# Attention with a softmax row passed through memory: when its reciprocals are taken, in what pieces they are written, and where the next weights are issued

## The reference

```python
scores = jnp.einsum('bhqd,bhkd->bhqk', q, k) / np.sqrt(Q_HEAD)
attn = jax.nn.softmax(scores, axis=-1)
o = jnp.einsum('bhqk,bhkv->bhqv', attn, v)
out = jnp.einsum('bhsv,Hv->bsH', o, Wo) + bo
```

## Time and profile before

| | |
|---|---|
| median of 3 runs | 3141.04 us (3134.56 to 3143.93) |
| the profiled execution, its own time | 3140.14 us |
| its span, first to last instruction | 3138.5 us |
| mean granted TensorE clock | 0.837 |
| PE busy | 2249.6 us (72%) |
| DVE busy | 1706.5 us (54%) |
| ACT busy | 1467.1 us (47%) |
| POOL busy | 516.1 us (16%) |

### The profile page before, as it was taken

How to read it: one execution, slowest core, us unless ns; L and a number is a source line. 1 busy time by engine, 2 the same in 40 slices (tenths; PEclk the granted TensorE clock), 3 DMA queues, 4 the chain that set the end, 5 groups by cost and what they waited for, 6 DMA issues and landing times. The chain is left out here.

```text
span 3138.5 us, 36938 instructions
## 1 busy us (share of the span) xinstructions
PE 2249.6 (72%) x11014; PEld 1759.9 (56%) x11014; DVE 1706.5 (54%) x2716; ACT 1467.1 (47%) x2616; POOL 516.1 (16%) x831
## 2 busy tenths in 40 slices
PE   8776767677776767676767677676767676676769
PEld 7555555555555555555655555555555555554557
DVE  6555555555555555554555555555555555554555
ACT  4454544444444445454444444444545444444434
POOL 3111111111111111111111111111211111111130
PEclk9888888878887888888888878887888888788789
DMA  5201010000001000101010010001010110101011
GB/s 205 74 21 26 21 26 21 22 25 21 27 20 27 20 27 20 26 21 26 22 24 24 21 26 20 27 20 27 21 27 21 26 21 20 27 20 26 18 56 45
DMA packets 123461, 95.20 MB, mean 30 GB/s; under 512 B 75008, under 2 KB 97568, under 8 KB 123424
## 3 DMA queue, kind: packets, MB, share of 16 engines
q1 hardware_dynamic: 119328, 86.33, 10.7%
q0 software_dynamic: 4096, 8.40, 1.0%
HBM read 83.95 MB, written 10.75 MB: 30 GB/s over the span
## 5 line engine op out<-in xcount | busy, mean ns | idle before, releaser
L766 ACT ACTIVATE PTH<-X 128x512 fp32r<-128x512 f32 x1024 | 565.7, 595 | 475.4 <-PE X L675 469.5
L817 DVE TENSOR_TENSOR PTL<-X,PTH 128x512 f16<-128x512 f32 x1024 | 664.6, 684 | 124.0 <-ACT PTH L766 119.8
L662 PE MATMUL O<-qaH,weff 128*128 128x512 f32 x128 | 100.2, 783 | 836.4 <-DVE onorm L849 822.1
L833 DVE TENSOR_REDUCE mx<-S 128x1 f32<-128x1024 f32 x512 | 622.9, 1217 | 57.8 <-PE S L695 57.5
L675 PE MATMUL X<-ident,prob 128*128 128x128 f32 x4096 | 628.9, 304 | 18.2 <-DVE PTL L817 15.6
L675 PEld LDWEIGHTS X<-ident,prob 128*128 128x128 f32 x4096 | 556.5, 160 | 144.5 <-issue 95.2
L849 DVE TENSOR_TENSOR onorm<-O,recip_row 128x512 f32<-128x512 f32 x128 | 88.5, 691 | 981.5 <-DMA recip_row<-row_scratch 981.5
L781 ACT ACTIVATE prob<-S,shift 128x1024 f32<-128x1024 f32 x512 | 572.1, 1117 | 0.0
L662 PEld LDWEIGHTS O<-qaH,weff 128*128 128x128 f32 x128 | 36.6, 286 | 890.1 <-DMA weff<-weff_scratch 797.4
L693 PE MATMUL S<-kvTH,qeH 128*128 128x512 f32 x1024 | 478.1, 467 | 1.6 <-DVE qeL L822 1.6
L798 ACT ACTIVATE onormH<-onorm 128x512 fp32r<-128x512 f32 x128 | 80.7, 631 | 805.0 <-DVE onorm L849 805.0
(11 more groups left out here) (201 smaller groups left out, 2139.4 us busy)
## 6 DMA issues: line engine op xcount, KB each, us to landing
recip_row<-row_scratch SPq DMA_DIRECT2D x128, 256.0 KB, 5.1
weff<-weff_scratch SPq DMA_DIRECT2D x128, 192.0 KB, 5.0
wv<-in_wv POOLq DMA_DIRECT2D x128, 64.0 KB, 2.1
raw<-in_raw SPq DMA_DIRECT2D x8, 772.0 KB, 6.6
weff_scratch<-w_split SPq DMA_DIRECT2D x8, 768.0 KB, 4.9
x<-in_x SPq DMA_DIRECT2D x4, 1024.0 KB, 6.8
x_all<-in_x SPq DMA_DIRECT2D x3, 1024.0 KB, 6.6
out<-y SPq DMA_DIRECT2D x3, 1024.0 KB, 4.2
```

Of the source, the lines that this page charges most:

```text
L662: mm(O[:], w[:, 0, :], keep["qaH"][:, tok], start=True, stop=False)
L766: nc.scalar.activation(PTH[p][:, part:part + 4, unit * P:(unit + 1) * P], X[:, k % 2, :].rearrange("p (k c) -> p k c", k=4), ACT.Copy).the ...
L817: v.tensor_tensor(PTL[p][at], X[:, k % 2, :].rearrange("p (k c) -> p k c", k=4), f32(PTH[p][at]), ALU.subtract).then_inc(low_out, 1)
L833: v.reduce_max(mx[:, col:col + 1], S[:, u % 2, :], AX.X).then_inc(max_ready, 1)
```

## The change

Four things change, all in `attention`:

1. DVE takes the reciprocals of head g-1 in quarter 1 of body g, in front of `low_q`, in place of quarter 2.
2. The scratch row is laid out by partition, then quarter (`"(p u) -> p u"`). Each partition's four numbers are now one piece of 16 bytes, 128 pieces, where there were 512 pieces of 4 bytes.
3. `onorm` reads `recip_row` in that layout: for a fixed quarter, its elements lie 16 bytes apart. `O` and `onorm` are addressed as before.
4. SP issues `load(g + 2)` in front of the wait for the reciprocals, not behind the read of the row.

```diff
             def body(g, b, h, par):
+                if exists(g + 2):
+                    load(g + 2, two_on[h] if not isinstance(g, int) else dram["weff_h"][(h + 2) % NH], par)
                 if exists(g - 1):
 
                     last = 1 - par
 
                     sp.wait_ge(recip_ready, g)
-                    with nc.allow_non_contiguous_dma(reason="512 numbers, turned from columns into a row"):
-                        sp.dma_start(dram["row"][last].rearrange("(u p) -> p u", p=P),
-                                     recip[:, last * UN:(last + 1) * UN]).then_inc(recip_out, 16)
+                    sp.dma_start(dram["row"][last].rearrange("(p u) -> p u", u=UN),
+                                 recip[:, last * UN:(last + 1) * UN]).then_inc(recip_out, 16)
                     sp.wait_ge(recip_out, 16 * g)
                     sp.dma_start(recip_row[last][:], dram["row"][last].partition_broadcast(P)).then_inc(row_in[last], 16)
-                if exists(g + 2):
-                    load(g + 2, two_on[h] if not isinstance(g, int) else dram["weff_h"][(h + 2) % NH], par)
...
-                        v.tensor_tensor(onorm[:], O[:], recip_row[par][:], ALU.mult).then_inc(onorm_ready, 1)
-                    if u == 1 and on and exists(g + 1):
-                        low_q(g + 1, h + 1 if not isinstance(g, int) else (h + 1) % NH, 1 - par)
-                    if u == 2 and one:
+                        v.tensor_tensor(onorm[:].rearrange("k (u p) -> k u p", u=UN), O[:].rearrange("k (u p) -> k u p", u=UN),
+                                        recip_row[par][:].rearrange("k (p u) -> k u p", u=UN), ALU.mult).then_inc(onorm_ready, 1)
+                    if u == 1 and one:
                         dve.wait_ge(probs_ready, 4 * g)
                         if not isinstance(g, int) or g >= 3:
                             dve.wait_ge(recip_out, 16 * (g - 2))
                         v.reciprocal(recip[:, (1 - par) * UN:(2 - par) * UN],
                                      rs[:, (1 - par) * UN:(2 - par) * UN]).then_inc(recip_ready, 1)
+                    if u == 1 and on and exists(g + 1):
+                        low_q(g + 1, h + 1 if not isinstance(g, int) else (h + 1) % NH, 1 - par)
```

## The result

The changed kernel takes 2000.7 us (1997.69 to 2001.29, 4 runs) where the kernel before took 3138.28 beside it: a ratio of 0.6372, 95% interval 0.6359 to 0.6385. The forecast was 2000. The span of the profiled execution is 1998.9 us.

A forecast was written before the change was run, and what follows sets the result against it. The row's chain, 22.7 us a head, would fall to 12.7, leaving PE's 13.66 as bound. With 0.14 added, 122.45 + 126 x 13.8, about 12, 124.4 and the small remainders give 2000 us; range 1970 to 2180.

The forecast's parts named there:

- What bounds: Waits for the row, `onorm` and `weff` are one gap; a head's period is a closed DVE, write, read, DVE chain, 22.71 us.
- The floor of 13.66 us: Sum of PE's four quarters at full clock: what a head costs where nothing waits for the row.
- The addition of 0.14: Added us per head for meetings of engines with little to spare, giving 13.8 us.
- The write: SP's write of the row to memory: 3.75 us with 128 pieces, between ends of 2.0 and 8.98.
- 2.0 + 7.0 / 4: The write's estimate: 2.0 us fixed, 7.0 us going with the pieces, of which a quarter remain.
- The read: Read of the row back from memory: unchanged at 5.1 us, between 3.2 and 5.6.
- The reciprocal's move: DVE's reciprocals in quarter 1 come 4.9 us earlier; their 0.17 us in front of `low_q` costs nothing.
- The load: Load of `weff` issued before the write: without that, its 797 us of waits become the next stall once the row is quicker.
- `onorm` with steps: `onorm` on DVE takes up to 1.06 us, not 0.69, but hidden; without cover 47 us in all.
- the copy's row: Profile row of a DVE copy spreading 512 elements by 16 bytes: 1.055 us against 0.684 plain; used to size `onorm`.
- The tail: From body 128's first transposes to the last `onorm`: about 12 us, where it was 26.1.
- a rival: Row still a little late: a write of 5 to 6 us gives 14.3 to 15.0 a head, about 2115 us; chance 0.12.

The follow-up runs named there:

- b_loadfront: The kernel before with only the load of `weff` moved in front of the write: 2989.94 us, ratio 1.0008.
- a_plain_onorm: The changed kernel with `onorm` reading the row without 16-byte steps, so reciprocals meet the wrong queries and only time counts: 1982.65 us, ratio 0.6322.
- x_spaced: The changed kernel plus one unread scratch write between write and read, 512 pieces of 4 bytes, 64 bytes apart: 2000.97 us, one execution.
- x_all16: The changed kernel plus one unread scratch write between write and read, 512 pieces of 4 bytes, 16 bytes apart: 2006.44 us, one execution.
- a_pieces4: The changed kernel with the write in 512 pieces of 4 bytes again and `onorm` without steps: 2467.48 us, ratio 0.7867.
- x_one: The changed kernel plus one unread scratch write of one column, 128 pieces of 4 bytes close together in 512 bytes: 2404.05 us, one execution.
- b_quarter1: The kernel before with only the reciprocals moved to quarter 1: 2340.37 us, ratio 0.7836, on a chip where the kernel before takes 2986.95.
- a_quarter2: The changed kernel with the reciprocals back in quarter 2, behind `low_q`: 1996.89 us, ratio 0.6368.
- a_loadback: The changed kernel with the load of `weff` back behind the read of the row: 2002.16 us, ratio 0.6382.

## Why the prediction was right

- *What bounds.* One chain, not three costs: right. b_loadfront shows it best: taking one of the three waits away changed its name and no time.
- *The floor of 13.66 us.* It was read from four quarters at full clock, two of them from the first heads. a_plain_onorm, where neither the row nor `onorm`'s steps are in the way, has transposes from body to body at (1844.00 - 122.47) / 126 = 13.66 us. The floor was right to 0.01.
- *The addition of 0.14.* Guessed, for meetings of engines in general, and the sum came out (13.80): that it did to the hundredth is luck. It now has a cause: at each of the 56 turns of the loop, with `onorm`'s longer time, 0.23 us in quarter 0 and 0.08 in quarter 1, or 56 x 0.31 / 126 = 0.14 a head.
- *The write.* 3.75 us forecast, 1.9 to landing and 1.44 of waiting measured, below the low end of 2.0. The step that failed is 2.0 + 7.0 / 4: it shared the time out by the number of pieces. The runs show closeness in its place. Memory completing 512 pieces, as the prediction had it, is not what the time goes with: 512 pieces at 64 bytes land in 2.6 us. That this didn't move the result is due to the slack, which is not large: 4.5 us from the write's issue to the read's gave 2001 us (x_spaced), 5.6 us gave 2006 (x_all16), both with a quicker read of 3.3 to 3.4.
- *The read.* 5.1 taken, 4.2 measured. It is longer (5.1) in a_pieces4, behind the close pieces. It does not simply follow the length of the write just ahead: in x_one that is 7.2 us and the read 3.5.
- *The reciprocal's move.* Its 4.9 us were sized rightly (5.05 in b_quarter1), and its new wait costs nothing. But the text let it stand as part of the gain. With the pieces of 16 bytes it brings nothing, since the chain is at the floor without it: a_quarter2. And its place in front of `low_q` is not quite free, as the prediction had it: 0.08 us in quarter 1 at each turn, 3.8 us between the two kernels.
- *The load.* Wrong. The prediction said that `weff` would become the next stall if the load kept its place. a_loadback shows no such stall. The step missed that the load follows the read, and that the read itself moves forward: it is issued 999.56 - 993.81 = 5.75 us behind the body's `onorm`, where it was 1507.03 - 1489.81 = 17.2.
- *`onorm` with steps.* The length was right (1.06 forecast, 1.07 measured), by the copy's row; "hidden" was not. With the turn of the loop it costs 2000.7 - 1982.65 = 18 us; 47 had been named as the price without cover. The cover was counted in a body inside the loop; at the turn it is shorter.
- *The tail.* About 12 us from the last body's transposes to the last `onorm`; 1874.4 - 1861.93 = 12.5 measured.
- *A slip in a rival.* A write of 5 us gives 3.84 + 5 + 5.1 = 13.9 us a head, not 14.3; only one of 6 us is clearly over the floor.

The Trainium skill, SBUF — State Buffer, section Specifications (TRN2), warned of a penalty for each new 16-byte line. The traces agree: `onorm` takes 1.07 us with the steps and 0.69 without, and that is what separates a_plain_onorm from the changed kernel. The Trainium skill, DMA: Bandwidth & Descriptors, section Anatomy of one DMA, written for the path that POOL issues, makes the receipt most of the fixed part and lets the fixed part scale with nothing. That most of such a write is spent behind its packets agrees with the earlier trace rows: they are gone by 1499.5, and SP goes on at 1507.03. That it scales with nothing does not hold for these writes, which SP issues: 1.44 to 8.98 us of waiting for at most 2 KB.

## What to carry to other kernels

When several engines wait for each other in a ring, follow the ring once from an instruction to its next occurrence and price each link; then compare with the period that the engines need without it. Whatever brings the chain under that floor brings everything, and the second and third such edit bring nothing, however well each is sized, and can cost a little: run them one at a time. And where columns must pass through memory, write what lies together in one piece; where that cannot be done, leave space between the pieces.

## What was not expected of the hardware

- A write of 0.5 KB in 128 pieces side by side took 7.2 us, and one of 2 KB in 512 pieces, 64 bytes apart, took 2.6.
- The long write differs between chips and the rest hardly: 8.98 us of waiting and 3138 us for the kernel before on one, 8.15 us (in b_loadfront) and 2987 us on another, with reads of 5.1 and 4.9 us, while kernels with quick writes stayed near 2001 on either.
- The read of the row was 5.1 us behind the close pieces, 4.2 behind pieces of 16 bytes, and 3.3 to 3.5 us where another write to a different scratch stood between. The load of `weff` right behind it, which reads other bytes, goes along: 5.0, 4.0 and 3.1 to 3.5 us. Whether reads are held up a while after a write of the same bytes has reported was not tested by itself.
- DVE stands for about half a us at a turn of a loop (27.5 us at 56 turns), without anything that the profile shows it to wait for.
